# Self-attention over image pixels on one core: the weighted sum's accumulator is copied out by ScalarE, and x is added by GpSimd

## The reference, cut to what matters

```python
xf = x.reshape(B, C, N)                       # B = 4 images, C = 256 channels, N = 1024 pixels
q = einsum('oc,bcn->bon', Wq, xf) + bq        # 32 rows
k = einsum('oc,bcn->bon', Wk, xf) + bk
v = einsum('oc,bcn->bon', Wv, xf) + bv        # 256 rows
attn = softmax(einsum('bqi,bqj->bij', q, k), axis=-1)
out = einsum('bcj,bij->bci', v, attn).reshape(x.shape) + x
```

## Time and profile before

| | |
|---|---|
| median of 3 runs | 168.96 us (168.79 to 169.66) |
| profiled execution, time | 169.59 us |
| its span, first to last instruction | 167.7 us |
| TensorE's granted clock | 1.0 of full |
| busy: PE, PEld, DVE | 160.9, 131.0, 139.1 us |
| busy: ACT, POOL | 108.0, 47.2 us |

### The profile page before, as it was taken

The page is one execution under the profiler, slowest core; times in us unless marked ns, Lnnn a source line. Parts: engine busy times, 40 slices in busy tenths (PEclk is TensorE's granted clock), DMA queues, the critical chain, the costliest instruction groups (busy, mean ns, idle before and its releaser), DMA issues. The chain is left out here.

```text
span 167.7 us, 2420 instructions
## 1 busy us (share of the span) xinstructions
PE 160.9 (96%) x781; PEld 131.0 (78%) x781; DVE 139.1 (83%) x221; ACT 108.0 (64%) x198; POOL 47.2 (28%) x63
## 2 busy tenths in 40 slices
PE   7898999999999999999999999999999999999992
PEld 4566888797887898788787898788787898876880
DVE  1879889899979999899979998898989879855353
ACT  3667896855997665767896655746896555754410
POOL 4229830080335300340335300250335300203500
PEclk9999999999999999999999999999999999999999
DMA  5923357054311230152310230052310230003003
GB/s 146 390 88 95 68 233 250 0 125 114 127 49 25 69 125 0 34 139 66 125 49 16 83 125 2 16 144 78 124 52 8 89 125 0 4 1 125 0 0 125
DMA packets 7660, 14.41 MB, mean 86 GB/s; under 512 B 1512, under 2 KB 1696, under 8 KB 7648
## 3 DMA queue, kind: packets, MB, share of 16 engines
q1 hardware_dynamic: 6528, 13.11, 23.9%
q0 software_dynamic: 832, 0.82, 2.3%
q10 hardware_dynamic: 288, 0.33, 0.6%
HBM read 4.52 MB, written 4.19 MB: 52 GB/s over the span
## 5 line engine op out<-in xcount | busy, mean ns | idle before, releaser
L826 PE MATMUL acc<-w_hi,v_hi 128*128 128x512 f32 x128 | 51.2, 400 | 0.0
L826 PE MATMUL acc<-w_hi,v_lo 128*128 128x512 f32 x128 | 50.3, 393 | 0.0
L434 ACT ACTIVATE w_full<-st 128x512 f32<-128x512 f32 x64 | 37.8, 593 | 10.5 <-PE st L812 10.5
L401 ACT ACTIVATE dump<-slot,negmax 128x1024 f32<-128x1024 f32 x29 | 32.4, 1118 | 13.2 <-DVE negmax L554 12.9
L834 PE MATMUL acc<-w_lo,v_hi 128*128 128x512 f32 x120 | 38.7, 398 | 0.3 <-POOL w_lo L330 0.2
L609 DVE TENSOR_TENSOR w_lo<-w_full,w_hi 128x512 fp32r<-128x512 f32 x48 | 33.1, 692 | 5.9 <-ACT w_full L434 1.6
L554 DVE TENSOR_REDUCE negmax<-slot 128x1 f32<-128x1024 f32 x29 | 35.3, 1216 | 1.6 <-PE slot L746 1.6
L330 POOL TENSOR_TENSOR w_lo<-w_full,w_hi 128x512 fp32r<-128x512 f32 x16 | 20.7, 1294 | 46.6 <-ACT w_full L434 46.5
L826 PEld LDWEIGHTS acc<-w_hi,v_hi 128*128 128x128 f32 x128 | 24.2, 189 | 7.1 <-DVE x_sb L618 1.2
L826 PEld LDWEIGHTS acc<-w_hi,v_lo 128*128 128x128 f32 x128 | 24.2, 189 | 5.3
L834 PEld LDWEIGHTS acc<-w_lo,v_hi 128*128 128x128 f32 x120 | 22.3, 188 | 7.0 <-POOL w_lo L330 2.0
(11 more groups left out here) (83 smaller groups left out, 188.1 us busy)
## 6 DMA issues: line engine op xcount, KB each, us to landing
out<-x_sb SPq DMA_DIRECT2D x7, 512.0 KB, 2.8
x_sb<-x SPq DMA_DIRECT2D x3, 1024.0 KB, 5.9
k_b<-k_a SPq DMA_DIRECT2D x8, 192.0 KB, 2.5
q_b<-q_a SPq DMA_DIRECT2D x8, 192.0 KB, 2.7
x_sb<-x SPq DMA_DIRECT2D x3, 256.0 KB, 4.2
k_a<-qk_parts SPq DMA_DIRECT2D x12, 64.0 KB, 2.1
q_a<-qk_parts SPq DMA_DIRECT2D x12, 64.0 KB, 2.3
out<-x_sb SPq DMA_DIRECT2D x2, 256.0 KB, 2.1
```

Source lines behind the costliest of these rows:

```text
L401: nc.scalar.activation(dump[:, t % 2, :], s_home(b, t), ACT.Exp, bias=negmax[:, t:t + 1], accum_out=rowsum[:, t:t + 1]).then_inc(rowsum_re ...
L434: nc.scalar.activation(w_full[:, r, :], st[:, j % 2, :], ACT.Exp).then_inc(exp_done, 1)
L826: nc.tensor.matmul(acc[:, c, :], v[:, b % 2, j, ch], w_hi[:, r, :], start=(j == 0 and v is v_hi), stop=False)
```

## The change

In all halves but the last (seven of eight) the accumulator is closed in two stages. ScalarE copies each bank with the bias into a new SBUF tile o_sb (take_out), which releases acc_read. GpSimd adds x (add_x) and signals a new semaphore, out_made; SP's send waits for that. VectorE's finish stays for the last half alone. ScalarE's take_out of a later half waits for out_made, since o_sb has one buffer.

```diff
+        o_sb = sb("o_sb", [P, CT, HALF])
...
             def send(b, h):
-                sp.wait_ge(acc_read, 2 * (2 * b + h) + 2)
+                sp.wait_ge(out_made, 2 * (2 * b + h) + 2)
...
+            def add_x(b, h):
+
+                for c in range(CT):
+                    pool.wait_ge(acc_read, CT * (2 * b + h) + c + 1)
+                    nc.gpsimd.tensor_tensor(x_sb[:, b, c, cols(h)], o_sb[:, c, :], x_sb[:, b, c, cols(h)],
+                                            ALU.add).then_inc(out_made, 1)
...
+                if n % JT == 2 and n >= JT:
+                    add_x((n - JT) // PER, (n - JT) // JT % 2)
                 if n % PER == JT + 5 and more:
                     send_rows(b + 1, 0)
                 split_w(n)
...
+            def take_out(b, h):
+                for c in range(CT):
+                    i = CT * (2 * b + h) + c
+                    if c == 0:
+                        act.wait_ge(acc0_ready, 2 * b + h + 1)
+                    else:
+                        act.wait_ge(av_done, PER * b + JT * h + JT)
+
+                    if i >= CT:
+                        act.wait_ge(out_made, i - CT + 1)
+                    nc.scalar.activation(o_sb[:, c, :], acc[:, c, :], ACT.Identity,
+                                         bias=bv_sb[:, c:c + 1]).then_inc(acc_read, 1)
...
                         if t % TH == TH - 1:
                             log_sums(b + image, t // TH)
+                    if s % JT == JT - 1 and (b, s) != (BATCH - 1, PER - 1):
+                        take_out(b, s // JT)
                     what, k, image = front(b, s)
...
-                    if s % JT == JT - 1:
+                    if (b, s) == (BATCH - 1, PER - 1):
                         for c in range(CT):
                             finish(b, s // JT, c)
```

More of the change, by code:

```diff
@@ L165, in nonlocal_attention @@
         acc_read = sem("acc_read")
+        out_made = sem("out_made")
         out_sent = [sem("out_sent0"), sem("out_sent1")]
```

## The result

The changed kernel takes 174.63 us (median of 4 runs, 174.61 to 174.80) against 168.88 us (168.64 to 169.66, 4 runs): a ratio of 1.031, 95% interval 1.0277 to 1.0343. The forecast was 174.6. The span of the profiled execution grew from 167.7 to 172.8 us, at full clock. All ratios here leave out two runs in which the granted clock was 0.858: one of the kernel before at 177.67 us and one of second_only at 186.49 us.

What follows compares the result with a forecast made beforehand. The prediction took TensorE's order of work as the bound, counting only time it is held up. 3 × 1.85 (handover plus later shift chain) + 0.1 = 5.65 us on a median of 168.96 gave 174.6, range 171.3 to 177.0.

Steps and rivals of the forecast that it cites:

- The handover: End of first halves (s = 7): ScalarE's copies start after sum_exp and free acc later, +1.0 us in images 0 to 2.
- The hold and the chain: First halves, images 0 to 2: adds hold VectorE's cast and subtraction; shifts and split_w 1.85 us later, w_lo wait +0.85.
- the weight loads' wait for split_w: Sign at the w_lo matmuls: TensorE's wait on GpSimd's split_w should grow from 2.0 us to 4 or more.
- The second halves: At s = 15: projections cover the copies, and VectorE's 1.4 us lead pays for the adds' hold, so 0.
- The last image: At n = 56, without sum_exp: bank 0 is free slightly later, +0.1 us; the tail stays the same.
- Rival 1: Handover alone: the adds hold nothing that TensorE comes to wait for; 172.1 us, chance 0.25.
- Rival 2: More than one add's worth: another 1.3 us reaches the shift chain in each of three images; 178.5 us, chance 0.09.
- Rival 4: No difference: copies cost nothing, or shorter waits at n = 29 repay the handover; within 0.8 us of 168.96, chance 0.06.
- Rival 3: Faster: freed VectorE brings row maxima, shifts and split_w sooner and handover waits vanish; 167.1 us, chance 0.05.

Runs made afterwards that it cites:

- second_only: Changed kernel with ScalarE and GpSimd closing only the second halves (s = 15) of images 0 to 2, VectorE all others: 169.99 us, ratio 1.002.
- copy_first: Changed kernel with ScalarE's two copies moved ahead of sum_exp in the step instead of behind it: 173.45 us, ratio 1.022.
- first_only: Changed kernel with ScalarE and GpSimd closing only the four first halves (s = 7), VectorE the second halves: 174.08 us, ratio 1.027.
- no_add: Changed kernel without GpSimd's adds, SP sending ScalarE's copy, so x is left out of seven of eight halves: 172.92 us, ratio 1.019.
- adds_late_send: Changed kernel with the first halves' adds four steps later on GpSimd and SP's send of that half moved to the image's end: 183.72 us, ratio 1.084.
- adds_first: Kernel before, finish still on VectorE, with two extra GpSimd adds into a spare tile in each first half: 171.27 us, ratio 1.011.

## Why the prediction was right

**The handover.** Forecast +1.0 in each of images 0 to 2. Measured 1.07, 1.52 and 1.09 more. The mechanism is the one forecast: the copies start at the end of sum_exp, and copy_first removes the loss by nothing but their place. The copies' length was well placed: the pair takes 1.26, where the forecast had 1.17, and the next instruction starts 1.14 after the first copy, where the forecast had 1.0. Two things were a little off. The forecast had TensorE no longer wait at bank 1, but in the second image its weight load there still waited 0.22 for the second copy, and the two starts take 0.53 (84.13 to 84.66) against 0.57 before. And 0.44 of the second image's 1.52 belongs to the second halves, below.

**The hold and the chain.** Forecast +0.85 at each w_lo matmul. Measured 0.41, 0.39 and 0.38. The unshown quantity, the subtraction beside an add, was taken from its upper side, and that was right: 1.60 and not 0.69. By the Trainium skill's rule of the lock on the shared pair of ports (its page "SBUF — State Buffer", section "SBUF: two separate sides") it had to be held, and the trace agrees. The term was mis-sized in adding up, by about half. In the third image the subtraction ended 1.60 later relative to TensorE's arrival and not 1.82: once the second add ended at 126.11 it needed 0.55 more, where I had put 0.85; the x_lo row of the kernel before would have given 0.55. And ScalarE closed up by 0.12 between the two sums (127.83 to 129.41, against 84.80 to 86.50). So the chain moved 1.49 and not 1.85, and TensorE had already lost 1.09 of it at the handover. Of the signs that the prediction named, this one was missed: the weight loads' wait for split_w grew from 2.0 to 3.2 us and not to 4 or more.

**The second halves.** Forecast 0. Measured 0.44 in the second image, and nothing in the third. The step that failed is "VectorE is 1.4 us ahead there, which pays for what the adds hold up". Into the second image it does not pay: VectorE had spent its time in hand on waits for ScalarE, 0.56 for the exponential and 0.44 for v_hi in second_only, before the held cast came. This is the 1.52 of the second handover, as first_only (1.30) and second_only (0.66) show from both sides.

**The last image.** Forecast +0.1, measured 0.11. The tail did not change.

The sum of 5.65 thus met 4.97: the hold was put 1.37 too large, the handovers 0.24 and the second halves 0.44 too small. That the median came out at the forecast is luck. The medians make 5.75 us of a growth that the spans have as 5.1. The times of the kernel before fall into two groups: beside the changed kernel three of its four runs took 168.6 to 169.0 and one 169.66, beside the experiments ten took 168.6 to 168.9 and 36 took 169.4 to 170.4. The forecast was set on a median of the lower group. Set against the profiled execution (169.59), which is of the upper one, it was 175.2, and the changed kernel's profiled execution took 174.65. What makes the two groups stays open.

Rival 1, handover alone, is refuted by the w_lo losses and by no_add. Rival 2 wanted another 1.3 us in each image at the w_lo matmuls, and they lost 0.4 more. Rival 4, no difference, is refuted by the time. Rival 3 needed ScalarE at bank 0 before 79.98. copy_first moved it ahead of sum_exp and still lost at the other end.

## What to carry to other kernels

Work taken off a busy engine gains only what the bounding engine waits for there. Ask in what order the new engine gets to it: here ScalarE stood in a 1.1 us instruction when TensorE wanted its bank. GpSimd instructions on SBUF are not free beside VectorE: look at which cast or two-input instruction falls under each, and follow what is queued behind it to the next engine that is short of time. When a signal comes later, look at every in-order queue that waits on it, the DMA queue too.

## What the runs showed of the hardware

A waiting VectorE cast got in between two GpSimd adds in the changed kernel (0.55 us, the second add stretched to 1.47), but behind three GpSimd instructions in a row in adds_late_send it waited for all, 3.62 us. What decides it was not tried; in the first case the second add began 0.22 after the cast did, in the second GpSimd had been at work 0.43 before the cast began. An add of a tensor to itself mostly took 1.03 us on GpSimd (adds_first), one of two tensors 1.29 to 1.75 (changed kernel). VectorE's v_lo, with one input in PSUM and one in SBUF, took 0.69 beside an add (second_only, at 100.25 us), as it does alone: it was not held. Three waits of 5.4 us each were each followed by TensorE at half its clock for 3 to 6 us. In adds_late_send, waits of about 1.5 and 0.8 us in quick succession were followed by starts 0.43 apart in the first and third images (granted clock 0.52 from 59 to 62 us), and not in the second, where the same two waits stand.
